# Two heads a bank pair for the exponentials, one head a bank for the maxima, and a select for the causal mask

## The chip, the cores and the metric

The kernel runs on one core of one Trainium2 chip. The metric is the device time of one execution in microseconds. The engines run their own instruction streams and meet at semaphores: TensorE (PE, with its weight loads as PEld), VectorE (DVE), ScalarE (ACT), GpSimd (POOL) and SyncE (SP), which here only issues DMAs.

## The reference

Two transformer layers over x of 4 x 512 tokens x 128. What matters here is the attention of each.

```
scores = einsum('bqhd,bkhd->bhqk', q, k) + einsum('bqr,bkr->bqk', q_rope, k_rope)[:, None]   # layer 0
scores = where(causal, -inf, scores / sqrt(8 + 32)); w = softmax(scores)
attn   = einsum('bhqk,bkhd->bqhd', w, v) @ W_o
...
attn   = softmax(einsum('bhnd,bhmd->bhnm', q * scale, k)) @ v                                # layer 1, no mask
```

There are 16 heads of 8 dimensions, 4 batch rows, 512 tokens. Layer 0 goes on with a dense mixture of 15 routed and 2 halves of shared experts, and layer 1 with a top-1 mixture of 8 experts.

## The kernel before

Attention runs as eight stages (layer L, batch row r). A stage has 4 groups G of 4 heads, and a group has 4 key tiles of 128: a quad Q is one key tile of one group, so a stage has 16 quads and a layer 64 (`NQ`). TensorE, VectorE, ScalarE each have an `attention(s)` loop over the quads in the same order, written out by hand.

*Maxima.* `max_unit(L, m)` on TensorE computes q k^T for one query tile `qt` and two heads into a pair of PSUM banks (`pairs[m % 2]`), and VectorE takes the row maxima with one TENSOR_REDUCE (L1496). A group has 8 units. A unit waits until the one two before it is taken. When a group's maxima are there, VectorE splits them (L1505, L1506), TensorE turns them (part `mt`), VectorE writes `mT`, and SyncE's `m_dma` puts them as two more operand rows beside q (L536), so that the exponentials' scores come out less their maxima.

*Exponentials.* `exp_unit(L, Q, j)` computes the transposed scores of one head and one key tile into a single bank (`singles[n % 2]`, L1082). ScalarE takes exp into one of 8 slots of `ring` (L881). A unit waits for the exponential two before it.

*Mask.* In layer 0 each score matmul, of maxima and exponentials alike, is followed by a bf16 matmul of the identity with a 128 x 128 mask of -1e30 into the diagonal tile (L1084).

*Values.* `values(L, Q)` multiplies the four heads' ring slots with `vaug` (v and a column of ones) into `p_o` (L1140). In quad Q+1 TensorE does it after the second exponent score:

```
for j in range(GH):
    exp_unit(L, Q, j)
    if j == 1:
        if Q:
            values(L, Q - 1)
        for name, b in beside_quad(s, q, "b"):
            part(name, b)
    else:
        for m in waiting[0:1] if j < 3 else waiting:
            max_unit(L, m)
        waiting = waiting[1:]
```

`S_AT` tells which maxima units stand in which quad: those of group G in the three (layer 0) or four (layer 1) of the quads 4G-6 to 4G-3. `TABLE` places the other parts (norms, q, k, v, projection, router) in the places "b" and "d" of a quad.

*GpSimd in layer 0.* `rope_copy(G)` spreads the rope rows to the 4 heads of q_op and k_op (L666, L667), and `weights0(n)` splits 10 pieces of the experts' weights into a rounded and a rest part (L673, L674), all at once where they come in its queue. SyncE loads these pieces (`expert0`), four in advance. In layer 1, `mask(G)` writes k_op (L747).

*SyncE.* One queue, in order: `head_dma`, `rope_dma`, `m_dma` and `expert0` stand in it in the order of the program, and each waits for its own condition. After attention 0 comes `dense()` (pairs for the hidden layer, singles[1] for the gates, singles[0] for the parts), and after attention 1 the expert blocks.

## Time and profile before

| | us |
|---|---|
| median of 3 runs | 988.91 (984.66 to 989.62) |
| profiled execution, its own time | 987.88 |
| its span, first to last instruction | 986.1 |
| PE busy | 817.1 (83%) |
| DVE busy | 657.8 (67%) |
| ACT busy | 521.0 (53%) |
| PEld busy | 519.6 (53%) |
| POOL busy | 289.5 (29%) |
| mean granted TensorE clock | 0.944 of full speed |

Busy time is the union of an engine's instructions over the span. Matmuls are pipelined and their ends modelled, so that a matmul's price is read from its start to the next one's start. DVE is VectorE, and POOL GpSimd. A span is about 1.8 us shorter than the execution's own time.

### The profile page before, as it was taken

To read this page: it belongs to the slowest core of one execution; us is meant where nothing else is said; L and a number is where in the kernel's file an instruction comes from. 1 tells how busy PE (TensorE), PEld (TensorE's weight loads), DVE (VectorE), ACT (ScalarE), POOL (GpSimd) and SP (SyncE) were. 2 spreads that over 40 slices of the span, in tenths; PEclk is the share of its full clock that TensorE was granted. 3 is DMA by queue.
4 is the path that set the end of the run, shared out by engine and by line. 5 is a ranking of instruction groups with operands and counts; after the bars stand their busy time and mean duration, and the time that the engine had idled before them with its cause. 6 is when DMAs were issued, how large, how long until landed. Compare 5 with 4: busy or idle time off the path is not lost. (4 is left out here: it accounts for less than half of the span.)

```text
span 986.1 us, 13424 instructions
## 1 busy us (share of the span) xinstructions
PE 817.1 (83%) x4532; PEld 519.6 (53%) x4532; DVE 657.8 (67%) x1354; ACT 521.0 (53%) x938; POOL 289.5 (29%) x227
## 2 busy tenths in 40 slices
PE   3567999999998899999989899789889999527850
PEld 2234555665564677777767644345444444226740
DVE  3135567676664586776867697688998886347852
ACT  1013455555546677777767626556556566317740
POOL 3452530311300100000004264772453452133425
PEclk9999999999999999999999969989999999859985
DMA  4253211111110292000002103210010100011003
GB/s 128 47 94 80 72 34 35 34 27 41 31 23 1 80 285 63 0 1 1 1 9 54 46 1 101 63 34 18 26 37 18 47 15 7 6 54 57 31 33 85
DMA packets 56415, 44.84 MB, mean 45 GB/s; under 512 B 6598, under 2 KB 47259, under 8 KB 56347
## 3 DMA queue, kind: packets, MB, share of 16 engines
q1 hardware_dynamic: 55323, 41.88, 16.3%
q0 software_dynamic: 1024, 2.10, 0.7%
q8 instruction: 36, 0.59, 0.2%
q14 instruction: 32, 0.26, 0.1%
HBM read 14.73 MB, written 14.55 MB: 30 GB/s over the span
## 5 line engine op out<-in xcount | busy, mean ns | idle before, releaser
L881 ACT ACTIVATE ring<-single 128x512 f32<-128x512 f32 (+3 forms) x512 | 255.6, 517 | 261.3 <-PE single L1084 143.6
L1496 DVE TENSOR_REDUCE mneg<-pair 128x2 f32<-128x1024 f32 (+3 forms) x256 | 259.6, 1022 | 84.4 <-PE pair L1084 55.7
L1082 PE MATMUL single<-q_op,k_op 104*128 104x512 f32 (+3 forms) x512 | 223.4, 449 | 15.5 <-ACT ring L881 10.7
L1082 PE MATMUL pair<-k_op,q_op 96*128 96x512 f32 (+3 forms) x512 | 185.3, 436 | 31.7 <-DVE mneg L1496 17.5
L747 POOL TENSOR_SCALAR k_op<-k_stk,cst 104x512 fp32r<-104x512 f32 x64 | 99.7, 1573 | 272.1 <-DMA k_stk<-hl 254.5
L1082 PEld LDWEIGHTS single<-q_op,k_op 122*128 122x128 f32 (+1 forms) x512 | 100.6, 197 | 91.6 <-ACT ring L881 65.0
L1082 PEld LDWEIGHTS pair<-k_op,q_op 120*128 120x128 f32 (+1 forms) x512 | 106.1, 212 | 49.2 <-DVE mneg L1496 25.0
L1140 PE MATMUL p_o<-ring,vaug 128*9 128x512 f32 (+3 forms) x1024 | 116.4, 527 | 0.9 <-ACT ring L881 0.9
L908 ACT ACTIVATE ring<-pair,cols 128x512 f32<-128x512 f32 x136 | 86.0, 684 | 35.3 <-PE pair L1184 29.6
L1551 DVE TENSOR_TENSOR ring<-ring,single 128x1024 f32<-128x1024 f32 x60 | 73.3, 1221 | 46.0 <-ACT ring L908 44.8
L1556 DVE TENSOR_TENSOR hid_lo<-ring,hid_hi 128x1024 fp32r<-128x1024 f32 x68 | 84.1, 1237 | 22.7 <-ACT hid_hi L923 19.7
L923 ACT ACTIVATE hid_hi<-ring 128x1024 fp32r<-128x1024 f32 x68 | 72.2, 1062 | 30.2 <-issue 29.4
L666 POOL CAST q_op<-qk_rope 96x2048 fp32r<-96x2048 f32 x12 | 22.7, 1890 | 143.8 <-ACT ring L881 64.4
L1084 PE MATMUL pair<-bfc,id_bf 128*128 128x128 bf16 x256 | 62.2, 243 | 0.0
L1084 PE MATMUL single<-bfc,id_bf 128*128 128x128 bf16 x256 | 59.8, 234 | 0.0
L1182 PE MATMUL pair<-h,w 128*128 128x512 f32 x136 | 56.5, 415 | 0.0
L1183 PE MATMUL pair<-h,w 128*128 128x512 f32 x136 | 54.4, 400 | 0.0
L1184 PE MATMUL pair<-h,w 128*128 128x512 f32 x136 | 54.2, 398 | 0.0
L1084 PEld LDWEIGHTS pair<-bfc,id_bf 128*128 128x128 bf16 x256 | 26.4, 103 | 23.3 <-issue 9.2
L1084 PEld LDWEIGHTS single<-bfc,id_bf 128*128 128x128 bf16 x256 | 25.2, 98 | 24.4 <-issue 12.3
L953 ACT ACTIVATE hid<-pair,b_blk 128x256 f32<-128x256 f32 x60 | 23.5, 475 | 11.4 <-PE pair L1255 11.4
L1184 PEld LDWEIGHTS pair<-h,w 128*128 128x128 f32 x136 | 26.4, 194 | 5.9
(293 smaller groups left out, 1301.1 us busy)
## 6 DMA issues: line engine op xcount, KB each, us to landing
xs<-zero SPq DMA_DIRECT2D x10, 1024.0 KB, 10.2
q_op<-hl SPq DMA_DIRECT2D x96, 64.0 KB, 2.0
stage<-in_L_ffn_W_dram SPq DMA_DIRECT2D x8, 512.0 KB, 4.4
stage<-in_L_ffn_rW_dram SPq DMA_DIRECT2D x6, 512.0 KB, 5.8
k_op<-hl SPq DMA_DIRECT2D x48, 64.0 KB
k_stk<-hl SPq DMA_DIRECT2D x48, 64.0 KB, 2.0
xb<-xs SPq DMA_DIRECT2D x15, 128.0 KB, 2.0
xs<-yb SPq DMA_DIRECT2D x15, 128.0 KB, 1.7
```

The source lines that it names most:

```text
L747: ins = pool.tensor_scalar(r32(k_op1[0:104, GH * ((G + 2) % 4) + j, :]), k_stk[0:104, g, :], cst[0:104, C_HM + j:C_HM + j + 1], None, ALU. ...
L881: exp_done.by(act.activation(ring[:, n % 8, lo:T], singles[n % 2][:, lo:T], ACT.Exp), (L, n))
L908: ins = act.activation(ring[:, k + c, :], pairs[v % 2][:, c, :], ACT.Gelu, bias=cols[:, R_B0 + 2 * u + c:R_B0 + 2 * u + c + 1])
L923: g_hi.by(act.activation(r32(hid_hi[:, i % 2, :, :]), ring[:, k:k + 2, :], ACT.Copy), i)
L1082: ins = pe.matmul(dst[:, lo:hi], r32(lhs[:, lhs_lo:lhs_lo + P]), r32(rhs[:, lo:hi]), start=True, stop=L == 1)
L1084: ins = pe.matmul(dst[:, diagonal:diagonal + P], id_bf[:, :], bfc[:, mask:mask + P], start=False, stop=True)
L1140: ins = pe.matmul(p_o[32 * j:32 * j + HD + 1, lo:T], vaug[:, (NB * L + G // NG) % 2, kc, GH * (G % NG) + j, :], ring[:, (GH * Q + j) % 8, ...
L1182: pe.matmul(pairs[v % 2][:, c, :], hi, r32(h[:, r, 0, :]), start=True, stop=False)
L1184: ins = pe.matmul(pairs[v % 2][:, c, :], lo, r32(h[:, r, 0, :]), start=False, stop=True)
L1496: s_taken.by(dve.tensor_reduce(mneg[:, G % 2, qt, 2 * p:2 * p + 2], pairs[m % 2][:, :, 0:hi], axis=AX.X, op=ALU.max, negate=True), (L, m))
L1551: gated.by(dve.tensor_tensor(both, both, singles[1][:, :].unsqueeze(1).broadcast_to([P, 2, T]), ALU.mult), v)
L1556: g_lo.by(dve.tensor_tensor(r32(hid_lo[:, i % 2, :, :]), ring[:, k:k + 2, :], hid_hi[:, i % 2, :, :], ALU.subtract), i)
```

## The change

Five things change, all in or around attention.

1. The exponentials use the pairs: a unit is half a quad, two heads, and ScalarE takes both banks with one ACTIVATE. The maxima use the singles: in layer 0 a bank holds both heads' 256 columns for the first two query tiles and one head for the others (12 units a group instead of 8), in layer 1 one head each (16 instead of 8).
2. In layer 0 the exponent scores have no mask matmul. Instead GpSimd sets the upper triangle of the diagonal tile in `ring` to zero after the exponential (`affine_select`, two heads at once, 128 in all), and the values wait for it (`cut`). The maxima keep their mask; two heads in one bank share one mask matmul.
3. In a quad's order, two maxima units stand between the two exponent units, the rest after part "b", and the values of the quad before come after them.
4. GpSimd's queue is laid out by half quads: after each select stands half a rope copy, or a third of a weight piece's split (cast, first half of the rest, second half of the rest).
5. SyncE's weight loads 4 to 9 are spread between the other DMAs, and some waits of the dense stage and the expert blocks follow the banks' new owners.

```diff
+SCORES = [[(heads, qt) for p in (0, 2) for heads, qt in (((p, p + 1), 0), ((p, p + 1), 1), ((p,), 2), ((p + 1,), 2), ((p,), 3), ((p + 1,), 3))],
+          [((j,), qt) for j in range(GH) for qt in range(NT)]]
+SU = [len(SCORES[L]) for L in range(2)]
...
-        spread = (((-5, (0, 1, 2)), (-4, (3, 4, 5)), (-3, (6, 7))), ((-6, (0, 1)), (-5, (2, 3)), (-4, (4, 5)), (-3, (6, 7))))[L]
+        spread = (((-5, range(0, 5)), (-4, range(5, 9)), (-3, range(9, 12))), ((-6, range(0, 4)), (-5, range(4, 8)), (-4, range(8, 12)), (-3, range(12, 16))))[L]
...
+WEIGHT_STEP = {at: n for n, at in enumerate([(0, k) for k in (*range(6, 16), *range(20, 24), *range(28, 32))]
+                                            + [(1, k) for k in range(4, 16)])}
...
+        def unit_scores(L, m):
+
+            heads, qt = SCORES[L][m % SU[L]]
+            return singles[m % 2][:, :].rearrange("p (i k) -> p i k", i=len(heads))
...
                 m_dma(0, G + 1)
+                head_dma(G + 3)
                 if r == 0:
-                    for n in range(4, 8):
-                        expert0(n)
-                head_dma(G + 3)
+                    expert0(4)
                 if r < NB - 1:
                     rope_dma(r + 1)
+                if r == 0:
+                    expert0(5)
                 m_dma(0, G + 2)
                 if r == 0:
-                    for n in range(8, len(PIECE0)):
-                        expert0(n)
+                    expert0(6)
                 if r < NB - 1:
                     head_dma(G + 4)
                 m_dma(0, G + 3)
+                if r == 0:
+                    expert0(7)
                 if r < NB - 1:
                     head_dma(G + 5)
+                    if r == 0:
+                        expert0(8)
                     m_dma(0, G + 4)
                     head_dma(G + 6)
+                if r == 0:
+                    expert0(9)
...
+            def cut_half(Q, half):
+
+                kc = Q % NT
+                exp_done.wait_ge(pool, (0, 2 * Q + half))
+                at = (GH * Q + 2 * half) % 8
+                tri = ring[:, at:at + 2, P * kc:P * (kc + 1)]
+                cut.by(pool.affine_select(tri, tri, [[0, 2], [1, P]], ALU.is_ge, fill, base=0, channel_multiplier=-1), (Q, half))
+
             for G in range(3):
-                rope_copy(G)
...
+                for w, half in ((0, 0), (0, 1), (1, 0), (1, 1)):
+                    rope_copy(G, w, half)
+            for r in range(NB):
+                for k in range(8 * NG):
+                    cut_half(4 * NG * r + k // 2, k % 2)
+                    if k < 4 and r:
+                        rope_copy(4 * r + 2, k // 2, k % 2)
+                    elif 16 <= k < 20 and r < NB - 1:
+                        rope_copy(4 * r + 4, k // 2 % 2, k % 2)
+                    elif 24 <= k < 28 and r < NB - 1:
+                        rope_copy(4 * r + 5, k // 2 % 2, k % 2)
+                    elif (r, k) in WEIGHT_STEP:
+                        n = WEIGHT_STEP[r, k]
+                        weights0(n // 3, n % 3)
+                    elif (r, k) == (2, 8):
+                        second_weights()
...
-                exp_done.by(act.activation(ring[:, n % 8, lo:T], singles[n % 2][:, lo:T], ACT.Exp), (L, n))
+                at = 2 * (n % 4)
+                exp_done.by(act.activation(ring[:, at:at + 2, lo:T], pairs[n % 2][:, :, lo:T], ACT.Exp), (L, n))
...
+                both = unit_scores(L, m)
+                for i, j in enumerate(heads):
+                    qs, ks = operands(L, G, j, 24)
+                    ins = pe.matmul(both[:, i, 0:hi], r32(qs[:, P * qt:P * (qt + 1)]), r32(ks[:, 0:hi]), start=i == 0 or L == 1 or qt >= 2, stop=L == 1)
+                    if L == 0 and qt >= 2:
+                        ins = pe.matmul(both[:, i, P * qt:P * (qt + 1)], id_bf[:, :], bfc[:, B_MS:B_MS + P], start=False, stop=True)
+                if L == 0 and qt < 2:
+                    ins = pe.matmul(both[:, :, P * qt:P * (qt + 1)], id_bf[:, :], bfc[:, B_MS:B_MS + P].unsqueeze(1).broadcast_to([P, 2, P]),
+                                    start=False, stop=True)
...
+                for i in range(2):
+                    qs, ks = operands(L, G, 2 * half + i, 26)
+                    ins = pe.matmul(pairs[n % 2][:, i, lo:T], r32(ks[:, P * kc:P * (kc + 1)]), r32(qs[:, lo:T]), start=True, stop=True)
+                st_full.by(ins, (L, n))
...
-                exp_done.wait_ge(pe, (L, GH * Q + GH - 1))
+                if L:
+                    exp_done.wait_ge(pe, (L, 2 * Q + 1))
+                else:
+                    cut.wait_ge(pe, (Q, 1))
...
+                    waiting = S_AT[L][Q]
+                    exp_unit(L, Q, 0)
+                    for m in waiting[0:2]:
+                        max_unit(L, m)
+                    exp_unit(L, Q, 1)
+                    for name, b in beside_quad(s, q, "b"):
+                        part(name, b)
+                    for m in waiting[2:]:
+                        max_unit(L, m)
+                    if Q:
+                        values(L, Q - 1)
                     for name, b in beside_quad(s, q, "d"):
                         part(name, b)
...
-                s_taken.by(dve.tensor_reduce(mneg[:, G % 2, qt, 2 * p:2 * p + 2], pairs[m % 2][:, :, 0:hi],
+                s_taken.by(dve.tensor_reduce(mneg[:, G % 2, qt, heads[0]:heads[-1] + 1], both[:, :, 0:hi],
                                              axis=AX.X, op=ALU.max, negate=True), (L, m))
```

VectorE's and ScalarE's `attention` follow the same order: two maxima units, part "b", the rest, part "d" on VectorE, and on ScalarE exp of half 0, part "b", exp of half 1, the copy of `p_o`, part "d". The first maxima unit of layer 1 now waits for `xy3` to be taken.

## Rows read from the trace of the kernel before

**Rows 1.** Busy time by stage: window, its length, PE, PEld, DVE, ACT, POOL (instructions), clock, DMA, GB/s
```profile
82.00:145.00 63.00, 59.73 (x433) 35.26 (x431) 38.95 (x78) 31.10 (x73) 28.85 (x22) 1.00 0.28 72
145.20:208.50 63.30, 61.43 (x453) 37.50 (x452) 44.77 (x127) 33.20 (x78) 11.19 (x6) 1.00 0.16 33
208.50:272.00 63.50, 61.58 (x454) 37.53 (x452) 43.82 (x119) 33.45 (x78) 11.20 (x6) 1.00 0.14 33
272.00:327.00 55.00, 48.30 (x366) 28.92 (x365) 27.17 (x81) 30.58 (x71) 0.20 (x1) 1.00 0.05 10
564.00:652.70 88.70, 79.51 (x330) 37.48 (x329) 67.67 (x103) 43.44 (x78) 54.54 (x36) 0.85 0.23 66
652.70:722.50 69.80, 62.96 (x331) 31.60 (x330) 62.17 (x152) 41.55 (x75) 32.00 (x24) 0.98 0.11 27
722.50:791.40 68.90, 61.56 (x331) 30.29 (x330) 61.41 (x146) 41.61 (x76) 32.63 (x24) 1.00 0.11 29
791.40:848.00 56.60, 50.84 (x276) 22.70 (x276) 37.34 (x107) 36.36 (x67) 17.57 (x14) 0.97 0.02 8
```

**Rows 2.** Waits, layer 1's middle stages (652.7 to 791.4): total us, times, longest
```profile
PEld single L1082 <- ACT ring L881: 15.9, 28, 0.9
...
PEld p_o L1140 <- ACT ring L881: 4.5, 13, 0.5
```

**Rows 3.** Waits, layer 0's middle stages (145.2 to 272)
```profile
PEld single L1082 <- ACT ring L881: 9.2, 19, 0.9
```

**Rows 4.** TensorE's timeline in layer 0: start us, duration us, instruction
```profile
205.34 0.36 PE L1082 MATMUL pair<-k_op,q_op 120*128 120x256 f32 x1
205.54 0.23 PE L1084 MATMUL pair<-bfc,id_bf 128*128 128x128 bf16 x1
205.58 0.36 PE L1082 MATMUL pair<-k_op,q_op 120*128 120x256 f32 x1
...
209.81 0.48 PE L1082 MATMUL pair<-k_op,q_op 120*128 120x512 f32 x1
...
210.17 0.47 PE L1082 MATMUL pair<-k_op,q_op 120*128 120x512 f32 x1
```

**Rows 5.** TensorE's timeline in layer 1
```profile
711.17 1.04 PE L1140 MATMUL p_o<-ring,vaug 128*9 128x512 f32 x8
...
712.51 0.63 PE L1082 MATMUL pair<-k_op,q_op 96*128 96x512 f32 x2
712.97 0.88 PE L1082 MATMUL single<-q_op,k_op 104*128 104x512 f32 x2
```

**Rows 6.** Instruction groups by shape, layer 0 (110 to 330): busy us, mean ns | idle before
```profile
L1496 DVE TENSOR_REDUCE mneg<-pair 128x2 f32<-128x1024 f32 x26 | 31.8, 1225 | 7.1 <-PE pair L1084 6.2
...
L1496 DVE TENSOR_REDUCE mneg<-pair 128x2 f32<-128x768 f32 x26 | 24.9, 956 | 2.8 <-PE pair L1084 2.3
...
L1496 DVE TENSOR_REDUCE mneg<-pair 128x2 f32<-128x512 f32 x26 | 17.9, 689 | 15.8 <-PE pair L1084 15.6
...
L1496 DVE TENSOR_REDUCE mneg<-pair 128x2 f32<-128x256 f32 x25 | 10.6, 423 | 8.7 <-PE pair L1084 8.5
```

**Rows 7.** Instruction groups by shape on GpSimd, whole span
```profile
L747 POOL TENSOR_SCALAR k_op<-k_stk,cst 104x512 fp32r<-104x512 f32 x64 | 99.7, 1573 | 272.1 <-DMA k_stk<-hl 254.5 <-issue 17.6
...
L667 POOL CAST k_op<-qk_rope 96x2048 fp32r<-96x2048 f32 x12 | 22.7, 1892 | 0.0
...
L674 POOL TENSOR_TENSOR w<-stage,w 128x1024 fp32r<-128x1024 f32 x6 | 14.1, 2356 | 0.5
...
L673 POOL CAST w<-stage 128x1024 fp32r<-128x1024 f32 x6 | 6.2, 1038 | 2.3 <-DMA stage<-in_L_ffn_rW_dram 2.3
...
L643 POOL TENSOR_SCALAR w_q<-raw 128x128 f32<-128x128 f32 x1 | 0.7, 651 | 0.1
```

**Rows 8.** VectorE's timeline in layer 1's lead
```profile
564.63 2.35 DVE L1496 TENSOR_REDUCE mneg<-pair 128x2 f32<-128x1024 f32 x2
567.16 2.36 DVE L1496 TENSOR_REDUCE mneg<-pair 128x2 f32<-128x1024 f32 x2 [0.18 <-PE pair L1082]
```

165 lines of the change are left out of this document (72 added, 93 removed).

## The prediction

> **What bounds the kernel now.** I read the busy time by stage first, because the change touches attention alone [rows 1]. The stage boundaries are the quads' value products at the starts of the attention stages. Layer 0's four stages take 63, 63.3, 63.5 and 55 us, layer 1's take 88.7, 69.8, 68.9 and 56.6. In layer 0 TensorE is busy for 61.4 of 63.3 us, VectorE for 44.8, ScalarE for 33.2, GpSimd for 11.2. So layer 0 is bound by TensorE, with a quad (one key tile of four heads) every 3.95 us. In layer 1 TensorE has 63.0 and VectorE 62.2 of 69.8 us: both are near the end of their room. GpSimd, which gets new work in layer 0, is nearly free from 145 us on but has the weight split before that (28.9 us in the first stage).
>
> The waits say how the two engines stall [rows 2, 3]. TensorE's loads wait for ScalarE's exponentials: 15.9 us at L1082 and 4.5 at L1140 in the two middle stages of layer 1 together, 9.2 at L1082 in those of layer 0. This is the ping-pong over two single banks, one head each.
>
> The dense stage and the expert blocks keep their instructions, and the loads ahead of the first quads their order, so I leave those stretches as they are.
>
> **Layer 0, TensorE.** Starts, not durations, give a matmul's price, because they are pipelined [rows 4]. A score of 256 columns with its mask takes 0.245 us (205.34 to 205.58), of 512 columns 0.36 (209.81 to 210.17), so one of 384 about 0.30. Without a mask behind it, a 512-column score takes 0.23 us: a pair's two at 712.51, the next instruction at 712.97 [rows 5]. The 256- and 384-column ones I put at 0.125 and 0.18, less 0.055 for each 128 columns, which is what the masked ones differ by.
> A group's 16 exponent scores are 8, 4 and 4 of these widths: 8 x 0.245 + 4 x 0.30 + 4 x 0.36 = 4.6 us before, 8 x 0.125 + 4 x 0.18 + 4 x 0.234 = 2.66 after, so 1.94 saved. The maxima of the first two query tiles now share one mask for two heads: 0.125 + 0.205 + 0.04 + 0.055 = 0.42 in place of 0.49, times 4 is 0.28. Together 2.2 us a group, 8.9 a stage.
> The bound on this from below: a mask's own start to the next score is only 0.04 us (205.54 to 205.58). If the other 0.1 us belongs to the score in this layer, whose operands have 122 rows, a mask saves 0.04, and a stage 2.6 + 1. I take 0.12, since layer 1's scores do without the 0.1.
>
> The waits for ScalarE also go, since a pair of scores now waits for an exponential a whole quad back. Layer 0 loses 2.5 us a stage by this, about half of the row's 4.6, because a weight load's idle time lies partly beside the running matmul.
>
> **What layer 0 gets in their place.** *Maxima in single banks.* There are 12 reductions a group instead of 8: 2 x (0.42 + 0.69) + 4 x 0.556 + 4 x 0.69 = 7.2 us against 2 x (0.42 + 0.69 + 0.96 + 1.22) = 6.58 [rows 6] (384 columns interpolated at 1.04 ns each). VectorE gets 2.5 us a stage, to 47.3, and stays under TensorE. But TensorE may be only one 0.6-us reduction ahead. By hand, in the quad with five units it reaches the third after 0.26 + 0.85 + 0.26 us, before the first reduction has ended, and ends at 3.8 instead of 3.05 us. The next two quads lose 0.3 and 0.2. That is 1.3 a group and 5 a stage. *Values moved to the quad's end.* The turn ot3 of the stage before follows them at once and waits for ScalarE's copy of p_o. A 512-column TensorE group and a ScalarE pass lie between; I estimate 1 us a stage. Sum of a stage: -8.9 - 2.5 + 5 + 1 = -5.4, so 57.9 us, 1.81 for half a quad.
> *GpSimd's select.* It cuts 256 columns twice a quad, and the values wait for it. The trace has none. From below, a copy is 0.92 ns a column (1892 ns for 2048): 0.36 us with 0.12 fixed. From above, two TENSOR_SCALAR of 128 columns at 651 ns: 1.3 us. L747, also one input and arithmetic, takes 1573 ns for 512 columns, which makes 0.8 us for 256 [rows 7]. I take 0.8, as the operation is nearest to that one.
> The Trainium skill (GPSIMD Engine Reference, section 3.1) puts a one-input loop at 1.03 to 1.8 cycles an element at 1.2 GHz. By that the select would be an estimated 0.22 to 0.38 us plus dispatch, and no half quad would be late; L747's row, at over 3 ns a column, says that the rule does not hold for all such operations.
> Beside the select, the same queue carries in 26 of the first stage's 32 half quads and 24 of the second's a step of the weight split (1.04 + 2.36 us in three steps for a piece of 1024, the smaller pieces less: 1.0 a step) or half a rope copy (0.95), and 0.1 for its waits. Such a half takes 0.8 + 1.0 + 0.1 = 1.9 us against TensorE's 1.81. Stage one: 26 x 1.9 + 6 x 1.81 = 60.3, less about 1.1 us by which a value product may lag; -4 of 63. Stage two the same, -4. Stage three has only bursts of four, which the lag takes up: -5.4. Stage four has no unit of a next group: -7.8 - 0.8 - 2.5 + 4 = -7. Layer 0: -20.5 us.
> SyncE's queue: the weight pieces now stand between the head and maxima rows, and each waits for a split. By the schedule the last one ahead of a maxima row waits for half quad 28, about when the row itself is made. I cost it at nothing as long as GpSimd keeps within one quad. What is late next, if it does not, is exp of the next stage's first group.
>
> **Layer 1.** No masks, no select. The exponentials' and the values' waits go. VectorE has 64 reductions of 0.69 instead of 32 of 1.22 a stage: +5 us, or +2.2 where they follow each other (2.35 for two, so 1.13 each from start to start [rows 8]). Its floor becomes 62.2 + 5 = 67.2 us. By hand a quad is six scores and maxima of 0.23, a wait of 0.3, a maximum, a wait of 0.35, a maximum, and the values at 1.04 [rows 5]: 3.55 us, and 0.4 of other parts, 63 us a stage. VectorE's floor is higher, so 67.2: -2.5 in each of the two middle stages. The last has VectorE busy 37 of 56.6 us. A middle stage's waits for ScalarE are 20.4 / 2 = 10 us [rows 2]; I take 7 for this one, give back 3 in banks, -4. The lead of layer 1 is a ping-pong at the slow clock, 2.54 us for two units from start to start [rows 8]; 16 one-head units at 0.78 take 12.5 us instead of 10, and the first must wait for xy3's addition, whose bank it uses: +3. The first stage itself runs at k_op's pace: 0. Layer 1: -6 us.
>
> ScalarE issues half as many, wider exponentials. It is idle for 30 of 63 us and 28 of 70 already [rows 1], so this gives nothing by itself.
>
> **Sum.** -20.5 - 6 = -26.5 on the profiled execution's 987.9 us, which is 1 us below the runs' median of 988.9. Forecast 963 us.
>
> **The rivals.**
> 1. *GpSimd sets layer 0's pace; slower.* Place: half quads 6 to 31 of stage one and all loaded ones of stage two, values behind cut. At 1.25 us a select, a loaded half is 2.35: stage one 72 us (+8), stage two 71 (+7), three -2, four -6, layer 1 -6: no gain, 989. This is the point from which it decides; at 1.5 us it is 62 x 0.25 = 15 more, 1004. For it: POOL is the slowest engine an element, and its arithmetic row is 3 ns a column. Against: the copy's 0.92. Chance 0.15.
> 2. *VectorE eats the gain in layer 1.* If each one-head reduction is followed by the 0.18 us idle that the lead shows, 64 x 0.87 = 56 us stand for today's 32 x 1.22 = 39, less 7.6 us of idle that exists (69.8 - 62.2): +9 in each middle stage, with the lead about +20 in all, so 983 to 988. For it: 89% busy. Against: two of them in a row have no idle time between them [rows 8]. 0.14.
> 3. *The masks were nearly free* (0.04 each): layer 0 gives 21 us less, 984. For it: the small gap [rows 4]; against it [rows 5]. 0.1.
> 4. *All hidden*: the select costs 0.4 us and other parts fill the waits for banks: layer 0 -36, layer 1 -8: 945. 0.11.
> The forecast's case, 948 to 978, has 0.5.
>
> **Range and chances.** 942 leaves out half of rival 4's lower side; 1000 leaves out the upper half of rival 1. The measurement tells 0.5%, 5 us. Faster: 0.5 + 0.11 + 0.1 of rival 2 + 0.05 of rival 3 = 0.76. Same 0.1, slower 0.14.
>
> **What would show it.** Right: starts of 0.13 us between exponent scores of 256 columns; no wait of TensorE for ScalarE; a layer 0 of 58 us stages with waits of TensorE for mneg; selects of 0.8 us and GpSimd near 95% in the first two stages; 128-column selects ahead of p_o in the waits. Wrong: a score still 0.2 us before the next (rival 3); p_o waiting for ring's select in every quad (rival 1); layer 1 stages over 70 us with VectorE full (rival 2); a maxima row's DMA late behind a weight piece on SyncE, which none of the terms has.

## The result and the profile after

The changed kernel takes 1007.05 us (median of 4 runs, 1002.16 to 1012.7) against 986.78 us of the kernel before in the same session: a ratio of 1.0197, 95% interval 1.0158 to 1.0236. It is slower by 20 us, where 963 and a range of 942 to 1000 were forecast. The profiled execution is the one of 1002.16 us, with a span of 1000.4. It is the shortest of the four, so its rows account for 14.3 of the 20 us (1000.4 less 986.1). The ratios below leave out an execution that is over 1.5% above the fastest of its kernel, which one of e9 is.

First the busy time by stage, in windows cut at the first value product of each stage, as in [rows 1]. Columns: window, its length, PE, PEld, DVE, ACT, POOL, granted clock, DMA share, GB/s.

```profile
83.20:142.50 59.30, 53.19 (x357) 30.47 (x360) 40.76 (x94) 27.19 (x42) 41.61 (x61) 0.97 0.34 77
142.50:213.60 71.10, 59.00 (x377) 35.38 (x380) 54.30 (x144) 28.83 (x46) 36.37 (x57) 0.93 0.13 30
213.60:280.00 66.40, 57.30 (x373) 33.56 (x372) 47.56 (x132) 28.59 (x46) 25.44 (x49) 0.95 0.15 32
280.00:323.00 43.00, 38.89 (x292) 22.25 (x290) 27.04 (x88) 22.45 (x38) 13.68 (x32) 1.00 0.06 11
591.30:662.80 71.50, 64.12 (x297) 30.18 (x300) 51.31 (x107) 36.06 (x40) 39.75 (x25) 0.95 0.24 68
662.80:737.90 75.10, 66.56 (x331) 32.55 (x330) 64.55 (x184) 37.63 (x43) 32.63 (x24) 0.98 0.10 26
737.90:811.30 73.40, 66.61 (x335) 32.63 (x338) 62.10 (x174) 37.51 (x43) 30.53 (x23) 0.98 0.11 27
811.30:861.90 50.60, 48.14 (x270) 21.66 (x269) 36.92 (x123) 30.38 (x34) 14.93 (x12) 1.00 0.02 7
```

Cut in the same way, to the end of the last value product, the kernel before has 63.1, 63.3, 63.5 and 51.8 us in layer 0, which is 241.7 against 239.8 after. In layer 1 it has 67.6, 69.8, 68.9 and 55.5, which is 261.8 against 270.6. The lead of layer 1, from VectorE's first maximum to the first value product, goes from 20.5 to 28.1 us. The dense stage and the expert blocks differ by under 1 us each, and layer 0 starts 1.1 us later. So the loss lies in layer 1, and the gain that layer 0 should have brought is missing.

What is to be seen in layer 0: TensorE is busy for 208.4 us where it was for 230.5. Its idle time has grown from 11.2 to 31.4 us, and the granted clock, which was 1.00 in all four stages [rows 1], is 0.97, 0.93 and 0.95 in the first three. Counting (1 - clock) x length as time lost to the clock gives 10.1 us, an estimate, and from above, as TensorE is also idle in part of that time. So 32 us of matmul work went, 20 came back as idle time and 10 as a slower clock.

The waits of layer 0's middle stages in the kernel after (142.5 to 280) say for whom TensorE waits: total, times, longest.

```profile
POOL ring L726 <- ACT ring L926: 74.8, 40, 6.1
...
PEld single L1153 <- DVE mneg L1545: 16.0, 27, 1.9
...
PE single L1153 <- DVE mneg L1545: 9.4, 14, 1.7
...
PE p_m L1098 <- DVE mrow L1555: 6.1, 6, 2.3
...
PEld pair L1172 <- ACT ring L926: 3.9, 5, 0.9
```

And in layer 1's middle stages (662.8 to 811.3):

```profile
PEld single L1153 <- DVE mneg L1545: 33.7, 64, 1.8
...
PE single L1153 <- DVE mneg L1545: 9.8, 15, 1.3
```

The waits of TensorE's score loads for ScalarE's exponentials are down to 3.9 us in layer 0's middle stages, where [rows 3] had 9.2, and to 0.9 in layer 1's, where [rows 2] had 15.9. In their place it waits for VectorE: for a maxima bank, and for the split of the maxima, mrow, that it is to turn. GpSimd waits for ScalarE before its selects, which are short. Instruction groups by shape on GpSimd, kernel after:

```profile
L726 POOL TENSOR_SCALAR_AFFINE_SELECT ring<-ring 128x256 f32<-128x256 f32 x128 | 52.6, 412 | 151.4 <-ACT ring L926 150.0
```

### The profile page after: what moved, and what is told of

Its sections match the earlier page's. It is cut to its first block and busy times, and to the rows that moved or that the text cites. A ratio compares the mean times of both kernels' runs of the same rounds, so it can differ in the third digit from the quotient of the medians.

```text
span 1000.4 us, 12903 instructions
## 1 busy us (share of the span) xinstructions
PE 806.9 (81%) x4212; PEld 506.5 (51%) x4212; DVE 687.3 (69%) x1546; ACT 486.9 (49%) x682; POOL 344.5 (34%) x389
## 5 line engine op out<-in xcount | busy, mean ns | idle before, releaser
L1545 DVE TENSOR_REDUCE mneg<-single 128x1 f32<-128x512 f32 (+2 forms) x448 | 274.3, 647 | 75.0 <-PE single L1153 28.4
L926 ACT ACTIVATE ring<-pair 128x1024 f32<-128x1024 f32 (+3 forms) x256 | 214.3, 863 | 227.6 <-PE pair L1172 227.0
L1153 PE MATMUL single<-k_op,q_op 96*128 96x512 f32 (+3 forms) x512 | 201.9, 452 | 58.3 <-DVE mneg L1545 40.0
L1172 PE MATMUL pair<-q_op,k_op 104*128 104x512 f32 (+3 forms) x512 | 166.1, 415 | 3.5 <-DMA q_op<-mT 2.5
L1153 PEld LDWEIGHTS single<-k_op,q_op 120*128 120x128 f32 (+1 forms) x512 | 101.7, 210 | 125.1 <-DVE mneg L1545 104.9
L1172 PEld LDWEIGHTS pair<-q_op,k_op 122*128 122x128 f32 (+1 forms) x512 | 86.6, 200 | 75.7 <-issue 48.4
L726 POOL TENSOR_SCALAR_AFFINE_SELECT ring<-ring 128x256 f32<-128x256 f32 x128 | 52.6, 412 | 151.4 <-ACT ring L926 150.0
L1155 PE MATMUL single<-bfc,id_bf 128*128 128x128 bf16 x128 | 31.5, 246 | 0.0
L685 POOL CAST q_op<-qk_rope 96x1024 fp32r<-96x1024 f32 x24 | 24.6, 1034 | 18.4 <-DMA qk_rope<-rope_hl 18.4
L997 ACT ACTIVATE hid<-pair,b_blk 128x256 f32<-128x256 f32 x60 | 23.5, 475 | 11.8 <-PE pair L1303 11.8
L1230 PEld LDWEIGHTS pair<-h,w 128*128 128x128 f32 x136 | 26.2, 193 | 5.6 <-issue 0.7
L1232 PEld LDWEIGHTS pair<-h,w 128*128 128x128 f32 x136 | 26.0, 191 | 5.7
## 6 DMA issues: line engine op xcount, KB each, us to landing
xs<-zero SPq DMA_DIRECT2D x10, 1024.0 KB, 10.2
```

The lines of the kernel that those rows point to most:

```text
L926: exp_done.by(act.activation(ring[:, at:at + 2, lo:T], pairs[n % 2][:, :, lo:T], ACT.Exp), (L, n))
L1153: ins = pe.matmul(both[:, i, 0:hi], r32(qs[:, P * qt:P * (qt + 1)]), r32(ks[:, 0:hi]), start=i == 0 or L == 1 or qt >= 2, stop=L == 1)
L1172: ins = pe.matmul(pairs[n % 2][:, i, lo:T], r32(ks[:, P * kc:P * (kc + 1)]), r32(qs[:, lo:T]), start=True, stop=True)
L1230: pe.matmul(pairs[v % 2][:, c, :], hi, r32(h[:, r, 0, :]), start=True, stop=False)
L1232: ins = pe.matmul(pairs[v % 2][:, c, :], lo, r32(h[:, r, 0, :]), start=False, stop=True)
L1545: s_taken.by(dve.tensor_reduce(mneg[:, G % 2, qt, heads[0]:heads[-1] + 1], both[:, :, 0:hi], axis=AX.X, op=ALU.max, negate=True), (L, m))
```

## The experiments

Ratios are to the kernel before on the same chip, with a 95% interval; differences between runs in us are differences of ratios times 988, unless medians are given. "Old banks" are the banks and the order of the kernel before. "New queues" are parts 4 and 5 of the change. e5, e9 and e11 leave the exponents' masking out altogether, so they do not compute the layer; they only price its parts.

| run | layer 0 | layer 1 | us | ratio |
|---|---|---|---|---|
| after | all of the change | new banks | 1007.1 | 1.0197 [1.0158, 1.0236] |
| e1 | all, values early | new banks, values early | 1007.2 | 1.0205 [1.0154, 1.0255] |
| e2 | old banks, new queues, select | old | 1001.7 | 1.0138 [1.0095, 1.0181] |
| e3 | new banks and queues, masks, no select | new banks | 1018.6 | 1.0312 [1.0268, 1.0357] |
| e4 | all of the change | old | 984.1 | 0.9962 [0.9928, 0.9997] |
| e5 | old banks, new queues, no mask, no select | old | 985.9 | 0.9979 [0.995, 1.0008] |
| e6 | old banks, new queues, masks and select | old | 1006.5 | 1.0205 [1.0156, 1.0253] |
| e7 | as e4, turns later | old | 993.4 | 1.0043 [1.0004, 1.0083] |
| e8 | as e7, values early | old | 988.3 | 1.0020 [0.9989, 1.0052] |
| e9 | old banks and queues, no mask, no select | old | 975.2 | 0.9855 [0.9831, 0.9878] |
| e10 | old banks, new queues, masks | old | 998.8 | 1.0094 [1.0062, 1.0127] |
| e11 | new banks, old queues, no mask, no select | old | 978.1 | 0.9896 [0.9862, 0.993] |
| e12 | as e4, each select twice | old | 994.6 | 1.0050 [1.0028, 1.0072] |
| e13 | as e4 | one-head maxima, four banks | 981.7 | 0.9937 [0.9908, 0.9966] |
| e14 | as e10, finer GpSimd instructions | old | 995.9 | 1.0090 [1.0063, 1.0117] |
| e15 | as e4, values early | old | 986.2 | 0.9984 [0.9957, 1.0011] |
| e16 | as e15, finer GpSimd instructions | old | 995.4 | 1.0088 [1.0055, 1.0121] |
| e17 | as e4 | one-head maxima, two banks | 1008.1 | 1.0218 [1.0168, 1.0268] |

### e1 to e4: the parts of the change

e1, the values back behind the second pair of scores:

```diff
                     exp_unit(L, Q, 1)
+                    if Q:
+                        values(L, Q - 1)
                     for name, b in beside_quad(s, q, "b"):
...
-                    if Q:
-                        values(L, Q - 1)
```

> The changed kernel with the values of the quad before moved back ahead of part b, right behind the second exponent unit. Theory A (the order): in the changed kernel the maxima's turn mt stands right behind two exponent units and finds the last reductions unfinished, about 1 us a group, and ot3 waits 1 us a stage; with the values in between, layer 0 loses 10 to 14 us and layer 1 about as much, total 980 to 990. Theory B (the banks): TensorE waits for VectorE over two single banks wherever the values stand; under 5 us gained, 1002 to 1007.

e2 keeps parts 2, 4 and 5 of the change and puts old banks and order back in both layers:

```diff
-                ins = pe.matmul(singles[n % 2][:, lo:T], ..., start=True, stop=L == 1)
-                if L == 0:
-                    ins = pe.matmul(singles[n % 2][:, P * kc:P * (kc + 1)], id_bf[:, :], bfc[:, B_MT:B_MT + P], ...)
+                ins = pe.matmul(singles[n % 2][:, lo:T], ..., start=True, stop=True)
```

> The kernel before with its banks and its order, but the exponent scores without their mask, GpSimd's select in its place, and the change's queues of GpSimd and SyncE. Theory A and B both: the select is hidden (0.41 us twice in 3.9), and 256 masks at 0.05 to 0.12 us go from the path of TensorE, layer 0 12 to 25 us shorter, total 962 to 975. Theory C (GpSimd's work itself slows VectorE's small operations and the values wait for the select): layer 0 as long as before or longer, 985 to 995.

e3 is the new kernel with the exponents' mask matmuls kept and `cut_half` left out. e4 is the new kernel with layer 1's banks, spread and order as before.

```diff
-                    cut_half(4 * NG * r + k // 2, k % 2)
```

> The changed kernel with the exponent scores' masks back and without the select: banks and order alone. Theory B: these are the loss, so layer 0 has the masks' TensorE time on top, total 1012 to 1025. Theory C: without the select VectorE's operations are fast again and the time falls, below 1002.

```diff
-SCORES = [NEW[0], NEW[1]]
+SCORES = [NEW[0], OLD]
```

> The changed kernel in layer 0, the kernel before in layer 1 (pairs for the maxima, singles for the exponentials, old order). Theories A and B: layer 1 gets its 15 to 16 us back, lead included, total 988 to 993. Rival D (the loss of layer 1 comes over from layer 0, by a later or colder start): under 8 us gained, above 999.

e1 measured 1007.19: the place of the values is not the cause. e4 measured 984.06, 4 us under the range of Theories A and B, so the new banks in layer 1 cost 1.0197 - 0.9962, or 23 us. This is more than the whole loss. e3 came out at 1018.6, as Theory B had it. e2 was the surprise: with nothing but the masks replaced by selects and the queues laid out anew, the kernel is 1.4% slower. Of the theories only C, in which GpSimd slows VectorE, went in this direction, and the time lies 7 us above its range too. Instruction groups on VectorE in e2's middle stages of layer 0 (150.1 to 286.7), and the same in the kernel before (145.2 to 272), fit C:

```profile
L1630 DVE CAST mrow<-mneg 128x16 fp32r<-128x16 f32 x8 | 5.7, 718 | 1.1
```

```profile
L1505 DVE CAST mrow<-mneg 128x16 fp32r<-128x16 f32 x8 | 1.4, 177 | 1.1
```

This cast of 16 columns is the first half of the split; a subtraction follows it, and then TensorE may turn the maxima.

### e5, e6, e9 to e12: layer 0 one factor at a time

e5 takes both the mask and the select out; e6 keeps both; e9 is the kernel before without the exponents' masks; e10 is the kernel before with the new order of GpSimd's and SyncE's queues alone; e11 is e9 with the new banks in layer 0. (The exponents have 256 mask matmuls; the 576 in e9's expectation is a slip.) The edits, in this order:

```diff
 e5  -  masks of the exponents, cut_half        (from e2)
 e6  +  masks of the exponents                  (from e2)
 e9  -  masks of the exponents                  (from before)
 e10 +  WEIGHT_STEP, expert0(4) to (9) spread   (from before)
 e11 +  SCORES[0], pairs for the exponents      (from e9)
```

> Old banks and order in both layers, the exponents' mask matmuls of layer 0 are left out and no select takes their place (so the masked exponentials are summed too: the output is not the reference's); the maxima keep their masks, GpSimd has only the weight and rope steps, which are no longer paced by selects. Theory S (the selects on GpSimd, one every half quad, stretch VectorE's short SBUF operations, and TensorE waits for the maxima's turn): without them layer 0 must show the whole price of the masks, some 64 groups x 1.0 to 1.5 us less the end effects, 935 to 965 us in all, VectorE's maxima cast back at 0.18 us and no wait of TensorE for the turn. Theory M (the masks' matmuls were nearly free, the selects too; what slows layer 0 in the runs with selects is the new pacing of the queues): 980 to 1000, like the run with the select alone.

> Old banks and order in both layers, the mask matmuls stay and the selects are done on top, on values that are already zero there: the suspected cost alone, without the saving. Theory S: the matmul stream is that of the kernel before plus the selects' hindrance, 12 to 25 us slower than the kernel before and slower than the run with the select alone by what the masks cost (together 1000 to 1025); VectorE's cast of the maxima stretches as in the select-alone run. Theory M: 985 to 1000, equal to the run with the select alone within 5 us.

> The kernel before with the exponents' 576 mask matmuls of layer 0 left out and nothing else: no select, and GpSimd's and SyncE's queues in their old order (rope copies in halves; the masked exponentials are summed too, so the output is not the reference's). Theory Q (the paced weight steps of the new queue order fall into the second stage and stretch VectorE there): the second stage is 60 to 62 us instead of 69.4, 968 to 978 in all. Theory W (the matmul stream is no longer what sets layer 0 once the masks are out: TensorE then waits for VectorE and ScalarE and the granted clock falls in these waits, whatever GpSimd does): stages as with the new queues, 982 to 990.

> The kernel before with nothing but the new order of GpSimd's and SyncE's queues (weight and rope steps in smaller pieces, staged through the first two stages); masks stay, no select. Theory Q: the second stage is 67 to 70 us instead of 63.3, 993 to 998 in all, and the run with masks and selects (1006) owes about half of its 18 us to it. Theory W: 985 to 990, as the kernel before, since TensorE has the masks' matmuls to do in the same time; all of the 18 us is then the selects' own.

> As the first kernel of this call (no masks of the exponents, no select, old queues) with the new banks and order in layer 0, the old ones in layer 1: what the pairs are worth when GpSimd has nothing new to do. The prediction's mechanism (pairs take away ScalarE's waits and single fixed costs): 5 to 10 us under the first kernel, 960 to 970. Theory W: within 4 us of the first kernel.

e12, from e4:

```diff
+                steps.step(pool.affine_select(tri, tri, [[0, 2], [1, P]], ALU.is_ge, fill, base=0, channel_multiplier=-1))
                 cut.by(pool.affine_select(tri, tri, [[0, 2], [1, P]], ALU.is_ge, fill, base=0, channel_multiplier=-1), (Q, half))
```

> New banks in layer 0 only (984.1 when each select is done once), each of the 128 selects done twice: the select's own price doubled. Theory S (selects hinder VectorE through the shared access and TensorE waits for the maxima's turn): 8 to 15 us slower, 992 to 1000. A theory that selects are nearly free and the losses come from the order of the queues and from waits: 984 to 989; only the wait of the values product for the select grows.

By their ratios: masks out, -14 us with the old queues (e9), -11 with the new ones (e5 less e10), -7 beside the selects (e2 less e6). New queues, +9 with the masks in (e10), +12 with them out (e5 less e9). Selects, +11 with the masks in (e6 less e10), +16 with them out (e2 less e5), +9 for the same number again (e12 less e4). The new banks in layer 0 add 4 where GpSimd does nothing new (e11 less e9, and the intervals overlap); beside the new queues without selects they are worth about -2 (e3 less e10, less layer 1's 23); and they bring 17 back where GpSimd has the selects (e4 less e2). The chain from before to after thus reads -14 + 12 + 16 - 17 + 23 = +20 us. The new queues cost about what Theory Q said: e9 is inside its range, e10 1 us above it. e5 fell in Theory M's range, but not for its reason: the masks are not free, as e9 shows; the new queues cost about as much as the masks give. e6's median is 5 us over e2's, which is Theory M's limit, and lies in Theory S's range: the selects cost, as S said, and beside them the masks cost only half of their 14 us. e12 lies in Theory S's range. e11, expected at 960 to 970 by the prediction's mechanism for the pairs, measured 978.1 and so refutes it for the pairs by themselves.

The cost of the queues lies in the second stage of layer 0. Windows of that stage in e9 and in e5, which differ in the queues' order alone (e9's profiled execution was its longest, 987.07 us against a median of 975.2, but this stage ran at the full granted clock):

```profile
143.20:204.70 61.50, 55.75 (x389) 32.04 (x388) 44.37 (x127) 32.94 (x78) 12.42 (x15) 1.00 0.17 36
```

```profile
141.60:211.00 69.40, 58.75 (x393) 34.43 (x396) 50.88 (x128) 33.08 (x78) 23.64 (x26) 0.93 0.16 35
```

VectorE has the same work and is busy for 6.5 us more while GpSimd has 11 us more to do; ScalarE's time is the same. The timelines of e10 at the start of this stage show how. First GpSimd's, then VectorE's, then TensorE's (start, duration, instruction):

```profile
146.02 1.28 POOL L737 TENSOR_TENSOR w<-stage,w 128x512 fp32r<-128x512 f32 x1
147.24 1.04 POOL L733 CAST w<-stage 128x1024 fp32r<-128x1024 f32 x1
148.36 1.28 POOL L735 TENSOR_TENSOR w<-stage,w 128x512 fp32r<-128x512 f32 x1
149.60 1.26 POOL L737 TENSOR_TENSOR w<-stage,w 128x512 fp32r<-128x512 f32 x1
```

```profile
146.12 1.20 DVE L1500 TENSOR_SCALAR nwtP<-nwtP 128x4 int32<-128x4 int32 x1
147.36 0.96 DVE L1667 TENSOR_REDUCE mneg<-pair 128x2 f32<-128x768 f32 x1
148.24 0.15 DVE L1504 SCALAR_TENSOR_TENSOR nwtP<-nwtP 128x4 f32<-128x4 f32 x1
148.42 1.24 DVE L1505 TENSOR_TENSOR nwtP<-nwtP 128x4 f32<-128x4 f32 x1
149.69 1.19 DVE L1506 SCALAR_TENSOR_TENSOR nwtP<-nwtP 128x4 f32<-128x4 f32 x1
```

```profile
155.18 0.37 PE L1178 MATMUL p_m<-cst,mrow 128*32 128x128 f32 x1 [5.71 <-DVE mrow L1677]
```

A VectorE instruction of four columns takes 0.15 us, or it takes 1.2 and ends when GpSimd's running instruction of 1.28 us ends (148.42 + 1.24 = 149.66; 149.60 is the start of GpSimd's next). The reduction out of PSUM between them takes its usual 0.96. Such steps stand ahead of the maxima's split in VectorE's queue, and TensorE, in order, stood for 5.71 us at the turn. The 30 short instructions on nwt and mrow in this stage take 5.0 us together in the kernel before, in e9 and in e11, 10.3 in e10, 11.3 in e5 and 12.0 in the kernel after. Part 5 of the change, which e10 has as well, is not what costs: TensorE's loads wait for rows from SyncE's queue (q_op<-mT) for 1.6 us in all of e10's layer 0, and for 1.2 in the kernel before.

The stall costs a second time, through the clock. TensorE stands from 149.5 to 155.2, and e10's windows before and behind 151.2 are:

```profile
145.20:151.20 6.00, 4.27 (x33) 1.98 (x32) 5.83 (x7) 2.57 (x6) 5.92 (x6) 1.00 0.41 50
151.20:161.40 10.20, 6.20 (x31) 4.51 (x32) 7.57 (x20) 1.32 (x4) 4.34 (x6) 0.50 0.02 4
```

The granted clock is at its lower level for 10.2 us. The kernel before, which has no idle stretch of TensorE of over 1.2 us in this stage, keeps the upper one.

The Trainium skill (SBUF — State Buffer, section "SBUF: two separate sides") says that VectorE and GpSimd share a port pair under an exclusive lock for a whole instruction, which a VectorE instruction needs in its two-port modes or with two SBUF inputs. These rows agree: three of the four-column instructions shown end within 0.05 us of the end of a GpSimd instruction, and the reduction out of PSUM is not touched.

### e14, e16: shorter GpSimd instructions

```diff
-                    steps.step(pool.tensor_copy(r32(w0[:, which, 0, lo:hi, :]), stage0[:, n % 4, 0:hi - lo, :]))
+                    cut_up(pool.tensor_copy, n, lo, lo, hi, 3)      # and so for the two subtractions; rope copies in four
```

> As the run with the new queue order alone (998.8), with each of GpSimd's weight operations cut in three and each rope copy in four, the same columns in shorter instructions. Theory P (a VectorE instruction on SBUF alone waits until GpSimd's running instruction has ended): the Newton steps of four columns in the second stage, 1.2 us there at their longest, are at most about 0.5 us, the stall of 5.7 us at the stage's start shrinks to 1 or 2, 990 to 994 in all. A theory that it is the amount of GpSimd's work (bandwidth shared in proportion) that stretches VectorE: their sum stays, 997 to 1001, or more for GpSimd's own fixed costs.

> The kernel before this one of the call with GpSimd's weight and rope operations cut in shorter instructions as well. Theory P: 973 to 979, the second stage back to 64 to 66 us, and the first version clearly under both kernels. The theory of shared bandwidth: 981 to 986.

VectorE's timeline in e14, at the same place:

```profile
143.29 1.51 DVE L1531 TENSOR_SCALAR nwtP<-mvP 128x4 f32<-128x4 f32 x1
...
145.04 0.96 DVE L1699 TENSOR_REDUCE mneg<-pair 128x2 f32<-128x768 f32 x1
145.92 0.39 DVE L1536 SCALAR_TENSOR_TENSOR nwtP<-nwtP 128x4 f32<-128x4 f32 x1
146.34 0.65 DVE L1537 TENSOR_TENSOR nwtP<-nwtP 128x4 f32<-128x4 f32 x1
147.03 0.67 DVE L1538 SCALAR_TENSOR_TENSOR nwtP<-nwtP 128x4 f32<-128x4 f32 x1
```

The steps behind the reduction take 0.67 us at most, the length of GpSimd's new pieces (2.82 us for four), and the stall at the turn is 3.56 us instead of 5.71. For these the wait is for the end of one GpSimd instruction, as Theory P has it. But the time is hardly better (995.9, between the two expectations): GpSimd is busy for 30.8 us of the stage instead of 23.5, and the 30 instructions still take 7.9 us.

And Theory P does not hold for all. The TENSOR_SCALAR at 143.29 took 1.51 us, through three whole GpSimd casts (143.47 to 144.78). e16, which its theories had at 973 to 979 and 981 to 986, measured 995.4, 9 us over e15. Its first stage takes 68.4 us instead of 58.5, and this is a part of it, VectorE first, then GpSimd, then TensorE:

```profile
117.65 4.03 DVE L1708 CAST mrow<-mneg 128x16 fp32r<-128x16 f32 x1
```

```profile
116.99 1.44 POOL L731 CAST k_op<-qk_rope 96x256 fp32r<-96x256 f32 x4
118.37 0.42 POOL L794 TENSOR_SCALAR_AFFINE_SELECT ring<-ring 128x256 f32<-128x256 f32 x1
118.75 1.29 POOL L744 TENSOR_TENSOR w<-stage,w 128x128 fp32r<-128x128 f32 x3
119.97 0.42 POOL L794 TENSOR_SCALAR_AFFINE_SELECT ring<-ring 128x256 f32<-128x256 f32 x1
120.35 1.29 POOL L744 TENSOR_TENSOR w<-stage,w 128x128 fp32r<-128x128 f32 x3
```

```profile
122.03 0.37 PE L1208 MATMUL p_m<-cst,mrow 128*32 128x128 f32 x1 [4.09 <-DVE mrow L1709]
```

A cast of 16 columns took 4.03 us, over eleven GpSimd instructions that follow each other without a gap, and ended at 121.68, with the last of them (121.64). A second one in the same stage took 3.18 us in the same way, and in e2's first stage, with GpSimd's instructions uncut, one took 2.16. So what such a VectorE instruction can wait for is GpSimd's whole gapless run, whatever the length of its pieces; that is longer than the one instruction of the rule given above, and the measurement decides. Cutting the pieces shorter does not help against it. When an instruction gets in between two of GpSimd's and when it does not, no run settles: in e10 two TENSOR_SCALARs got in after one. Of the 9.9 us that e16's first stage is longer, 3.8 are TensorE's idle time and 6.1 its busy time, at a granted clock of 0.88 instead of 0.99.

### e7, e8, e15: the order around the turn

e7 moves mt0 to mt3 from part "b" to part "d" of their quads; e8 also puts layer 0's values early; e15 is e8 without the first.

```diff
-          (2, "b"): ["mt1", "P.ne"], (2, "d"): ["T.proj"],
+          (2, "b"): ["P.ne"], (2, "d"): ["mt1", "T.proj"],
```

> New banks in layer 0 only, as in the run of that kind (984.1), and the four transposes of the maxima (mt0 to mt3) moved from the middle of their quad to its end, behind the values product. Theory S says TensorE stands about 1 us at each of them while VectorE's cast and subtraction are late: 16 x 0.6 to 1 us come back in layer 0 (and some in layer 1, where it waits too), 968 to 976. Theory M, and a theory that the clock or the banks set layer 0's length: 981 to 987, the wait only moves to the next instruction.

> As the run before, with the values product of layer 0 placed right behind the second pair of the exponents' scores, as the old order had it. Theory S: the transposes come even later and the values product no longer covers them in the same way, 968 to 978, within 4 us of the run before. A theory that the order of layer 0 cost part of its time (the values product at the end of the quad delays the exponents' buffers): 3 to 6 us under the run before.

> New banks in layer 0 with the values product right behind the second pair, old banks in layer 1. By the stages of the run with the values early in both layers (58.8, 68.3, 63.7, 47.3 against 59.3, 71.1, 66.5, 43.0 of the new kernel): 980 to 984, 2 to 3 us under the same kernel with the values at the quad's end. A theory that the order does nothing in layer 0: 984.

Theory S missed in e7 and e8, and so did its rival in e7. The turns moved back made it 9 us slower by the medians (993.4 against 984.1), not 8 to 16 faster. The values' place in layer 0 gives 5 us back with the late turns by the medians (e8), 2 by the ratios, whose intervals overlap, and makes no difference that can be told without them (986.2 against 984.1, 2 us above both of e15's theories).

### e13, e17: what layer 1 pays for

Both have the exponents' old banks and order in layer 1 and one-head maxima in the banks of the pairs. They differ in one thing:

```diff
-                return pairs[m // 2 % 2][:, m % 2:m % 2 + 1, :]     # e13: four banks, wait for unit m - 4
+                return pairs[m % 2][:, 0:1, :]                      # e17: two banks, wait for unit m - 2
```

> Layer 0 as in the new kernel; layer 1 with its old banks and exponents (one head in each single bank), but its maxima taken one head at a time, each in one bank of the pairs, so that four units can be ahead instead of two. The new kernel's layer 1 costs some 20 us over the old one (984.1 with the old). Theory F (the price is VectorE's: 256 reductions of 0.69 us for 128 of 1.22, and its queue is full): nearly all of it is here too, middle stages of 73 to 75 us, 998 to 1006. Theory D (the price is the depth: with two single banks TensorE and VectorE wait for each other at each unit): with four banks it is gone, 984 to 990.

> As the run with one-head maxima on four banks (981.7), but on two banks only (the first of each pair), so that a unit waits for the reduction two units back, as in the new kernel; the exponents keep their old banks and order. Theory D (the depth of the maxima's ring is what layer 1 pays for): it comes back here, lead of 27 to 28 us, middle stages of 73 to 75, 996 to 1004. Theory E (the price comes from the exponents in pairs, their order and the values at the quad's end): the maxima's depth does nothing by itself, 981 to 986.

e13: 981.7 us, 2 under Theory D's range. e17: 1008.1, 4 above it, and 28 more than e13 by the ratios. Against e4, whose layer 1 is the old one throughout, e17 costs 25 us, and the whole new layer 1 costs 23. Middle stages of layer 1 and their waits of PEld, e13 and then e17:

```profile
641.40:711.80 70.40, 64.39 (x331) 31.99 (x330) 64.05 (x185) 41.68 (x76) 31.63 (x24) 0.95 0.10 26
711.80:780.40 68.60, 62.22 (x331) 30.24 (x330) 62.48 (x177) 41.63 (x76) 32.16 (x23) 1.00 0.11 29
```

```profile
PEld pair L1266 <- DVE mneg L1699: 5.1, 10, 1.1
```

```profile
655.30:732.70 77.40, 69.91 (x331) 31.78 (x330) 64.88 (x184) 41.79 (x76) 32.91 (x24) 0.93 0.10 26
732.70:808.40 75.70, 69.09 (x334) 30.73 (x335) 63.53 (x178) 41.84 (x76) 31.92 (x24) 0.95 0.10 26
```

```profile
PEld pair L1266 <- DVE mneg L1699: 24.0, 54, 1.4
```

VectorE is busy for the same 64 us in both, so it is not what sets the stage's length. Theory D holds and Theory F falls: the doubled number of reductions costs next to nothing with four banks. The price is the depth: how many units TensorE may be ahead of VectorE. It falls mostly on TensorE's busy figure: 64.39 us become 69.91 with the same 331 matmuls, about 2 us of it by the clock (0.93 instead of 0.95), the rest probably because the modelled end of a pipelined matmul counts as busy wherever none follows at once. TensorE's idle time grows by only 1.5 of the stage's 7.0 us, so idle time alone would have hidden most of this wait. The lead of layer 1 is 19.8 us in e13 and 24.0 in e17, so of the kernel after's 28.1 the depth accounts for about 4 us; what the rest is no run separates.

## Why the prediction was wrong

Two steps failed. In layer 1 the forecast took the larger of two floors, 63 us of TensorE's stream and 67.2 of VectorE's, where the waits between the two engines over only two banks come on top of both. In layer 0 it had no term for what GpSimd's work does to VectorE's short instructions, nor for the clock. By e4, layer 0 with all of its changes brings 4 us (0.9962) where 20.5 were forecast, and layer 1 costs 23 where 6 were to be gained. The prediction's steps in order:

- **The select**, taken at 0.8 us between 0.36 and 1.3, is 412 ns, at the lower bound. Rival 1's condition (1.25 us) is not met, and GpSimd does not set the pace: it is busy for 70% of the first stage and 51% of the second, where near 95% was the sign. But the text asked only how long GpSimd's own queue takes. What its work does to VectorE beside it has no term in the sum, and it is 9 to 12 us for the new queues and 9 to 16 for the selects. In the second stage VectorE is busy for 54.3 us where 47.3 were forecast, and the short instructions are 7.0 us longer.
- **Masks.** The matmul work saved was nearly right: in e5, busy time falls from 230.5 to 213.2 us in layer 0, and 8.7 more are the clock's by the formula above, so 26.0 us or 1.62 a group, 0.10 a mask, against 1.94 and 0.12. With the shared masks of the maxima the whole saving is 32 us against 34.5 expected. The sign that was named for it did not come: two exponent scores of 256 columns that follow each other in a pair start mostly 0.20 us apart, not 0.13, which was rival 3's sign (the two at 187.50 below take 0.47 to the next instruction), and two of 512 columns 0.33, not the 0.234 taken over from layer 1. A mask behind a score of 256 columns costs only 0.04 us from start to start, and a part of the 0.10 lies elsewhere: the maxima's scores of 256 columns take 0.17 us to the next instruction in e9's middle stages, and 0.21 in the kernel before's. Rival 3 (masks nearly free) is wrong as to TensorE's work, and yet e9's kernel gains only 14 us. Its two middle stages show why, at the full granted clock before and after: busy time falls by 11.6 us, idle time grows by 8.4, and 3.2 are gained.
- **Waits for ScalarE** are mostly gone from the middle stages, as said. **ot3** behind the values costs TensorE 0.9 us of idle time a stage, where 1 was put. The maxima's rows are not late behind the weight pieces on SyncE: TensorE's loads wait for them for 2.8 us in all of layer 0.
- **Maxima in single banks.** This is the step that failed, first in layer 1: "By hand a quad is six scores and maxima of 0.23, a wait of 0.3, a maximum, a wait of 0.35 ... 63 us a stage. VectorE's floor is higher, so 67.2". The middle stages are 75.1 and 73.4, at 64.6 and 62.1 us of VectorE: the floor was even put too high, and neither engine is full, TensorE idle for 8.5 and 6.8 us and VectorE for 10.6 and 11.3. e17 against e13 shows the mechanism with its size, 28 us. The hand count let only reductions stand between a bank's filling and its release. VectorE's queue has other parts between them, and the bank ring holds only so much of VectorE's time: two one-head units are 2 x 0.68 = 1.4 us of reductions, two old pairs 2 x 1.22 = 2.4, four one-head units 2.7. TensorE can't run ahead over a part that is longer than the rest of this. The prediction had seen the ring's shallowness in layer 0 and put it at 5 us a stage. In layer 1, where VectorE's queue is fullest, it had the waits only inside the 63 us that it then dropped for the larger 67.2.

A place in layer 0 of the kernel after shows one such wait, VectorE first and then TensorE:

```profile
187.49 1.02 DVE L1545 TENSOR_REDUCE mneg<-single 128x2 f32<-128x256 f32 x2
188.43 0.16 DVE L1504 COPY topk<-top 128x12 f32<-128x12 f32 x1
...
190.07 0.22 DVE L1516 TENSOR_TENSOR gate<-gate,gate 128x64 fp32r<-128x64 f32 x1
190.21 1.01 DVE L1545 TENSOR_REDUCE mneg<-single 128x1 f32<-128x384 f32 x2
```

```profile
187.50 0.48 PE L1172 MATMUL pair<-q_op,k_op 122*128 122x256 f32 x2
187.97 0.44 PE L1153 MATMUL single<-k_op,q_op 120*128 120x384 f32 x1
...
188.85 0.23 PE L1155 MATMUL single<-bfc,id_bf 128*128 128x128 bf16 x1
190.81 0.51 PE L1153 MATMUL single<-k_op,q_op 120*128 120x512 f32 x1 [1.73 <-DVE mneg L1545]
```

Twelve short routing instructions stand between two reductions for 1.8 us; both banks are full, TensorE stops, and the exponents' scores and the values behind it stop too.

- **The clock** had no term. It was 1.00 in all of layer 0, and the forecast kept it there. The kernels after and e13 have the same program in layer 0 and idle times of 31.4 and 30.6 us there, but other granted clocks. The second and third stage of e13:

```profile
140.50:208.80 68.30, 56.21 (x373) 32.88 (x372) 53.99 (x144) 28.84 (x46) 36.31 (x57) 0.98 0.14 31
208.80:271.70 62.90, 54.48 (x378) 32.03 (x380) 46.90 (x133) 28.53 (x46) 25.54 (x49) 1.00 0.16 33
```

At 0.98 and 1.00 instead of 0.93 and 0.95 they are 2.8 and 3.5 us shorter; over all of layer 0 it is 232.9 against 239.8 us. So in this execution the clock's part was some 7 us (8.7 by the formula above, 10.1 less 1.4), and it varies between executions of this one layer. In the kernel after the clock falls to its lower level three times inside layer 0's stages, at 147.6, 192.0 and 256.9, each time within 2 us of the end of an idle stretch of TensorE (2.28 us from 144.6, 1.73 from 189.1, 1.68 from 255.4). e13 has the same three stretches, and only the first is followed by a fall; the kernel before has one of 1.82 us from 104.4 and no fall. e2 and e6, the selects without and with the masks' matmuls, have granted clocks of 0.86, 0.90, 0.97, 0.90 and of 0.90, 1.00, 1.00, 1.00 in layer 0, but e2's profiled execution is 7 us over its median, so the 1.3 us between their layers 0 are not its usual difference. That the idle stretches cause the falls is argued from these rows; no run changed the idle time and nothing else.

- **Stages of layer 0**: first -3.8 (-4 expected), second +7.8 (-4), third +2.9 (-5.4), last -8.8 (-7). The last was nearly right. The first was right by luck: its -4 came from GpSimd setting the pace at 1.9 us a half quad, which it did not do. In layer 1 the lead was +7.6 (+3), the first stage +3.9 (0), the last -4.9 (-4).
- **The rivals.** Rival 2 named about the size of layer 1's loss ("about +20 in all"). It was right that VectorE stands idle between one-head reductions, 10.6 and 11.3 us in the middle stages against 7.6 and 7.5 before, but put it down to the reductions' number, with VectorE full; e13 has the same number on four banks, and its middle stages are 4.7 and 4.8 us shorter. It also left layer 0's 20 us of gain standing.

What stays open: how much of the selects' 9 to 16 us is VectorE's waiting beside GpSimd and how much the clock; e12 and e6 give the sum only. Why the new banks bring 17 us in layer 0 beside selects and nothing without them was not separated; that a pair's exponential is waited for a quad later, which leaves the select room, is a guess. e9's 14 us can't be laid out by stage, as none of its usual executions was profiled. And no version kept e9's 14 us: the best that compute the whole are e13 (0.9937) and e4 (0.9962), whose intervals overlap, 0.4 to 0.6% under the kernel before.

## What to carry to other kernels

Measure a buffer ring's depth in microseconds of its consumer's work, not in buffers, and compare it with the longest run of other instructions in the consumer's queue: two banks of one-head units instead of four cost 28 us here, while the doubled count of instructions cost nothing. Two engines of which neither is full can still set a stage's length together. Before moving work to an idle GpSimd, look which short VectorE instructions on SBUF lie on a chain that TensorE waits for; each can take as long as GpSimd's running instruction, or as its run of instructions without a gap. When matmul work is removed from an engine that is 97% busy, write down who is next in each stage and what its idle time was, since half of the removed time may come back as waits.

## What the runs showed of the hardware

- VectorE instructions of four columns took 0.15 us or 1.2 us, the rest of GpSimd's 1.28 us instruction (e10); when GpSimd's pieces were 0.7 us, those of the second stage took 0.67 at most, but one just ahead of it 1.51 (e14). Reductions out of PSUM kept their 0.96 us. With selects and weight steps beside it, the cast of the 16 maxima took 0.72 us on average in e2 (0.18 before).
- Such a cast took 4.03 us in e16, to the end of a run of eleven GpSimd instructions without a gap.
- One-head units on two banks instead of four made layer 1's middle stages 7.0 and 7.1 us longer, and TensorE's modelled busy time 5.5 and 6.9 us longer with about the same matmuls (e17, e13).
- A select over 256 fp32 columns takes 412 ns on GpSimd, near the 0.36 us that its copy's rate gives [rows 7] and far from the 3 ns a column of its TENSOR_SCALAR.
- The granted clock of layer 0 differed between the kernel after and e13, which have the same program there (0.93 and 0.98 in the second stage), with the same idle time of TensorE within 1 us in all of layer 0. Behind a stall of 5.71 us it was at its lower level for 10.2 us (e10).
